# Row maxima by two heads at a time on half of the array, in a written-out cycle

## What is computed

```python
q = (x @ q_w + q_b).reshape(Bx, Tx, NH, HD).transpose(0, 2, 1, 3)
k, v = (kv[0], kv[1])
att = jnp.einsum('bhqd,bhkd->bhqk', q, k) * (1.0 / np.sqrt(HD))
att = att + build_alibi_bias(NH, Tx)[None]
att = jnp.where(causal[None, None], att, -jnp.inf)
att = jax.nn.softmax(att, axis=-1)
y = jnp.einsum('bhqk,bhkd->bhqd', att, v)
return y.transpose(0, 2, 1, 3).reshape(Bx, Tx, Cx) @ o_w + o_b
```

## Time and profile before

| | |
|---|---|
| median of 3 runs | 2727.81 us (2725.26 to 2729.4) |
| the profiled execution | 2729.97 us, span 2727.9 us |
| mean granted clock of TensorE | 0.978 |
| PE busy | 2598.3 us, 95% of the span |
| DVE busy | 2321.1 us, 85% |
| ACT busy | 2059.8 us, 76% |
| POOL busy | 1373.4 us, 50% |
| DMA | 299.58 MB moved, mean 110 GB/s |

### The profile page before, as it was taken

One profiled execution on the slowest core, in us unless ns is written; L12 is line 12 of the kernel. 1 busy time (PEld: TensorE's weight loads), 2 busy tenths in 40 slices (PEclk: granted clock), 3 DMA queues, 4 the chain that ended last, 5 costly groups with the idle time before them and its releaser, 6 DMA issues.

```text
span 2727.9 us, 57513 instructions
## 1 busy us (share of the span) xinstructions
PE 2598.3 (95%) x21670; PEld 1637.9 (60%) x21670; DVE 2321.1 (85%) x4175; ACT 2059.8 (76%) x3887; POOL 1373.4 (50%) x1768
## 2 busy tenths in 40 slices
PE   6779999999997999999999999999999999999998
PEld 4569989999996444545445454454544545455454
DVE  3468888888886998999989998899998999999993
ACT  2248878877884687888887887788887887887886
POOL 2235555555653365464654645546464464654644
PEclk9889999999998899999999999999999999999999
DMA  2015575545555646556474564655546556474540
GB/s 73 1 44 171 179 189 186 173 164 177 176 178 165 106 74 123 80 99 106 73 127 75 104 105 68 122 82 98 100 79 122 82 97 102 77 127 77 103 89 17
DMA packets 315172, 299.58 MB, mean 110 GB/s; under 512 B 97174, under 2 KB 265516, under 8 KB 314668
## 3 DMA queue, kind: packets, MB, share of 16 engines
q1 hardware_dynamic: 313344, 295.55, 50.9%
q10 hardware_dynamic: 1552, 0.36, 0.1%
HBM read 175.27 MB, written 120.06 MB: 108 GB/s over the span
## 4 chain that ended last, share of the span: by engine, by line
PE 54%; ACT 6%; DMA 5%; issue 1%; SPq 0%; DVE 0%; POOL 0%; POOLq 0%; ACTq 0%
PE t_y L1570 19%; PE t_r L1554 16%; PE t_a L1505 12%; ACT t_prob L1599 6%; DMA scr_m<-t_mrows 4%; PE t_a L1538 4%; PE t_r L1516 3%; DMA t_q<-scr_m 1%; DMA t_k<-t_blockb 0%; DVE t_mxc L1647 0%; ACT t_mrows L1616 0%; SPq L1411 0%; ACT t_near L1608 0%; SPq L1417 0%; POOL t_prob L1744 0%
## 5 line engine op out<-in xcount | busy, mean ns | idle before, releaser
L1599 ACT ACTIVATE t_prob<-t_r 128x512 f32<-128x512 f32 (+1 forms) x2432 | 1261.4, 599 | 289.5 <-PE t_r L1554 285.4
L1647 DVE TENSOR_REDUCE t_mxc<-t_a 128x1 f32<-128x512 f32 (+3 forms) x1920 | 1129.3, 643 | 105.4 <-PE t_a L1505 102.7
L1554 PE MATMUL t_r<-t_q,t_k 109*128 109x128 bf16 (+4 forms) x4608 | 831.7, 275 | 31.1 <-DMA t_q<-scr_m 20.9
L1505 PE MATMUL t_a<-t_k,t_q 99*128 99x512 bf16 (+3 forms) x2560 | 650.1, 320 | 1.5 <-DVE t_mxc L1647 1.0
L1750 POOL TENSOR_SCALAR_AFFINE_SELECT t_near<-t_near 128x512 f32<-128x512 f32 x512 | 332.7, 650 | 532.3 <-ACT t_near L1608 532.1
L1570 PE MATMUL t_y<-t_prob,t_v 128*32 128x512 f32 (+3 forms) x6144 | 588.0, 496 | 0.0
L1554 PEld LDWEIGHTS t_r<-t_q,t_k 102*128 102x128 bf16 (+1 forms) x4608 | 373.6, 98 | 342.9 <-ACT t_prob L1599 133.1
L1744 POOL TENSOR_SCALAR_AFFINE_SELECT t_prob<-t_prob 128x512 f32<-128x512 f32 x512 | 322.5, 637 | 276.9 <-ACT t_prob L1599 276.9
L1608 ACT COPY t_near<-t_r 128x512 f32<-128x512 f32 x512 | 307.5, 602 | 82.6 <-PE t_r L1516 65.6
L1505 PEld LDWEIGHTS t_a<-t_k,t_q 99*128 99x128 bf16 x2560 | 210.8, 98 | 228.5 <-DVE t_mxc L1647 155.0
L1570 PEld LDWEIGHTS t_y<-t_prob,t_v 128*32 128x32 f32 x6144 | 157.7, 109 | 257.3 <-issue 182.4
(11 more groups left out here) (199 smaller groups left out, 4129.2 us busy)
## 6 DMA issues: line engine op xcount, KB each, us to landing
t_q<-scr_q SPq DMA_DIRECT2D x384, 128.0 KB, 4.0
t_k<-scr_k SPq DMA_DIRECT2D x384, 128.0 KB, 6.6
scr_q<-j_part SPq DMA_DIRECT2D x96, 256.0 KB, 3.4
scr_k<-j_part SPq DMA_DIRECT2D x96, 256.0 KB, 2.5
scr_v<-j_v SPq DMA_DIRECT2D x32, 544.0 KB, 5.0
t_v<-scr_v SPq DMA_DIRECT2D x64, 272.0 KB, 8.1
p_x<-in_x SPq DMA_DIRECT2D x32, 512.0 KB, 4.3
scr_res<-j_x SPq DMA_DIRECT2D x32, 512.0 KB, 3.8
```

The lines of the kernel that those rows point to most:

```text
L1505: mm = pe.matmul(abank[n % A_BANKS][:, x * w:(x + 1) * w], q_op[t % NG][0:KA, h0 + x, i * P:(i + 1) * P], k_op[t % NG][0:KA, h0 + x, k0:k0 ...
L1554: mm = pe.matmul(ring[n % RING_BANKS][:, s * w + lo:s * w + hi], k_op[g][0:deep, h0 + s, j * P:(j + 1) * P], q_op[g][0:deep, h0 + s, q0 + ...
L1599: nc.scalar.activation(prob[:, q % SLOTS, h0:h0 + m, 0:w], ring[n % RING_BANKS][:, 0:m * w].rearrange("p (h n) -> p h n", h=m), ACT.Exp).t ...
L1647: V.tensor_reduce(mxc[:, t % 2, k0 // 512, h0:h0 + m, i], abank[n % A_BANKS][:, 0:m * w].rearrange("p (h n) -> p h n", h=m), AX.X, ALU.max ...
```

## The change

In `attend`, and in what the earlier stages lay ready for it:

- **Max and diag become one.** `q_max` and `k_max` are new operands: heads 0 and 1 of the group on partitions 0 to 62, heads 2 and 3 on 64 to 126. They hold three position rows, three of the six products of parts (48 rows, NMAIN = 51) and 12 rows of marks (NMAX = 63), whose product gives a large negative number where a key lies behind its query. A unit is a pair of matmuls, one for each half of the array's rows, into two banks of PSUM, and one reduction of up to 1024 elements. A group has 19 units: 15 of 1024 elements and 4 of 768. No copy by ACT, no select by POOL, no reduction from SBUF.
- **PSUM:** two slots of two banks for the maxima, in place of three of one; three banks in the ring, in place of four.
- **The maxima rows** go through ACT's own queue: `lift` issues the write, `spread`, some exponents later, waits for it to land and issues the read.
- **scale** goes from DVE to POOL; join is one operation, not two.
- **Order:** PE follows `CYCLE`, a table of 73 pieces that is run through once for each group (the four `out` once for each batch). `late` is how many periods a piece stands behind. The costs are used for the other engines' order only.
- **Loads:** three sets of operands, not four. q, k and v as before (12 transfers of 128 KB and one of 272 KB in a group), plus `q_pos` and, for the maxima, 12 transfers of 64 KB. The first group's are issued in `project`, 38 transfers in place of 18. `prepare` builds the marks on POOL.

```diff
-A_BANKS, RING_BANKS, SLOTS = 3, 4, 6
+A_SLOTS, RING_BANKS, SLOTS = 2, 3, 6
+BUFS = 3
+CYCLE = (
+    ("exp", 25, 9), ("exp", 26, 9), ("weigh", 2, 9), ("weigh", 3, 9), ("rows", 0, 8), ("exp", 27, 9),
...
             def largest(t, u, n):
-                i, k0, w, h0, m = MAX_UNITS[u]
-                if u == 0:
-                    operands_in(t)
+                pieces, pair = MAX_UNITS[u]
+                if first_max[t] == n:
+                    pe.wait_ge(s_qk[t % BUFS], 16 * (MARKS + MAX_LOADS * (t // BUFS + 1)))
                 free_slot(n)
...
+                        for depth, lo, hi in ((NMAIN, 0, far), (NMAX, far, w)):
+                            if lo < hi:
+                                for e in range(2):
+                                    mm = pe.matmul(abank[n % A_SLOTS][:, 512 * e + at + lo:512 * e + at + hi],
+                                                   q_max[t % BUFS][64 * e:64 * e + depth, h, i * P:(i + 1) * P],
+                                                   k_max[t % BUFS][64 * e:64 * e + depth, h, k0 + lo:k0 + hi],
+                                                   start=True, stop=True)
...
-                nc.scalar.copy(mrows[:, :], abank[n % A_BANKS][:, :].bitcast(BF16)[0:3 * GH * QT, 0:P]).then_inc(s_al, 1)
+                nc.scalar.copy(mrows[:, :], abank[n % A_SLOTS][:, 0:512].bitcast(BF16)[0:3 * GH * QT, 0:P]).then_inc(s_al, 1)
+                act.wait_ge(s_al, t + 1)
+                act.dma_start(scr["m"][t % NG], mrows[:, :]).then_inc(s_mw, 16)
+
+            def spread(t):
+                act.wait_ge(s_mw, 16 * (t + 1))
+                if t >= BUFS:
+                    act.wait_ge(s_pv, NQ * (t - BUFS + 1))
+                act.dma_start(q_op[t % BUFS][KA:KB, :, :].rearrange("p h t -> p (h t)"),
+                              scr["m"][t % NG].rearrange("(s n) q -> s (n q)", s=3)).then_inc(s_m[t % BUFS], 16)
```

More of the change, by code:

```diff
@@ L99, in prepare @@
         ones = sb("p_ones", [P, P])
+        marks = [sb(f"p_mark_{n}", [MSUB, P]) for n in "qk"]
         ldT = sb("p_ldT", [100, 4])
@@ L1174, in settle, with cyclic @@
                 e[4](end)
+def cyclic():
+    order = []
+    for period in range(min(e[2] for e in CYCLE), GROUPS + max(e[2] for e in CYCLE)):
+        for place, (kind, x, late) in enumerate(CYCLE):
+            t = period - late
+            if 0 <= t < GROUPS and (kind != "out" or t % NG == NG - 1):
+                order.append((period + place / len(CYCLE), kind, t // NG if kind == "out" else t, x))
+    return order
 def plan():
-    lead, lag = 1.5, 0.12
     pl = Planner()
-    width = [KEY_QUADS[r][3] * per_bank(KEY_QUADS[r][3]) for r, h0 in PIECES]
@@ L1196, in plan @@
-    streams = {n: list(reversed(s)) for n, s in streams.items()}
     slot_freed, ring_freed = [], []
     def maxima_in(t):
-        if all(("max", t, u) in pl.done for u in range(NU)) and all(("reduce", t, i) in pl.done for i in range(QT // 2)):
-            pl.give("DVE", max(pl.when("reduce", t, i) for i in range(QT // 2)), t - lead + 1, ("join", t, 0), 320,
-                    lambda end: pl.give("POOL", end, t - lead + 1, ("split", t, 0), 1250))
-    def selected(t, i, end):
-        if i % 2 == 1:
-            pl.give("DVE", end, t - lead + 0.5, ("reduce", t, i // 2), 1141, lambda end: maxima_in(t), "reduce")
+        if all(("max", t, u) in pl.done for u in range(NU)):
+            pl.give("DVE", max(pl.when("max", t, u) for u in range(NU)), t - 0.5, ("join", t, 0), 180,
+                    lambda end: pl.give("POOL", end, t - 0.5, ("split", t, 0), 1250))
@@ L1208, in weighted, with lifted @@
+    def lifted(t, end):
+        pl.issue.append((end, "lift", t, 0))
+        pl.give("ACT", end + 4000, t - 0.5, ("spread", t, 0), 330)
     def weighted(t, c, end):
@@ L1212, in inverted @@
         def inverted(end):
-            pl.give("DVE", end, t + 0.5, ("scale", t, c), 370, scaled)
+            pl.give("POOL", end, t + 0.5, ("scale", t, c), 720, scaled)
         def swapped(end):
-            pl.give("DVE", end, t + 0.5, ("invert", t, c), 290, inverted)
+            pl.give("DVE", end, t + 0.5, ("invert", t, c), 220, inverted)
         pl.give("DVE", end, t - 0.5, ("swap", t, c), 620, swapped)
@@ L1290, in plan @@
             slot_freed.append(("lift", t, 0))
-            pl.give("ACT", now + 165, rank, ("lift", t, 0), 200, lambda end, t=t: pl.order["SP"].append(("lift", t, 0)))
+            pl.give("ACT", now + 165, rank, ("lift", t, 0), 530, lambda end, t=t: lifted(t, end))
         elif kind == "exp":
@@ L1309, in plan @@
                 weighted(t, LAST_QUAD.index(x), now + 180)
-            if x == NQ - 1 and t + NG < GROUPS:
-                pl.order["SP"].append(("load", t, 0))
+            if x == NQ - 1 and t + BUFS < GROUPS:
+                pl.issue += [(now + 3000 * z, "load", t, z) for z in range(LOAD_PIECES)]
         elif kind == "out":
```

437 lines of the change are left out of this document (221 added, 216 removed).

## The result

The changed kernel takes 2766.09 us (median of 4, 2755.74 to 2772.86), the kernel before on the same chip 2728.61: 1.013 times as long, 95% interval 1.0089 to 1.0171. The forecast was 2654, 2.7% less, with a range of 2575 to 2745. It was wrong, and on the wrong side. The profiled execution took 2762.49 us with a span of 2760.0. Of all executions in this document one, of experiment e6 (2918.57 us), was in a slower state of the chip and is left out of its ratio.

A forecast was written before the change was run, and what follows sets the result against it. TensorE was taken as the bound, with VectorE close behind. First lift at 922 us, 62 groups of 26.9 (25.99 of TensorE work plus 0.9 of waits), then 17.7, 31 and 15.5 gave 2654 us; range 2575 to 2745.

The forecast's parts named there:

- the rows' part: Maxima rows' write and read on ScalarE's queue: median write landed before the wait, 3.4 us against 4.2 us of exponents.
- a DMA share of at most 0.77: Transfers of a group: 3.6 MB in 26.9 us, 134 GB/s, sets this upper limit on the DMA engines' share.
- Rival C: Wait for the maxima write holds ScalarE 1.8 us if landing grows to some 6 us; 28.2 a group, 2735 us, chance 0.08.
- the one for all waits: Waits in a group: about 0.5 us for the maxima rows and 0.4 for banks, 0.9 in all (0 to 1.8).
- TensorE's sum: TensorE's own work for one group of the changed kernel, matmuls and array changes: 25.99 us.
- the 0.5 for narrow pairs: Maxima on TensorE: 0.5 us a group, between nothing and 1.1, for the 20 pairs that are 128 wide.
- Rivals A and B: Maxima on TensorE: changes to halves cost 0.24 us, 2852, chance 0.14; or halves don't run at once, 2870, chance 0.05.
- Its terms gave 26.54: TensorE's own work for one group of the kernel before: 26.54 us of the 28.38 a group took.
- 1.08 a group: TensorE in the kernel before: waits for maxima rows not yet back, 22.8 us in 600; about 0.5 expected after.
- Half of the matmul time that the halves save is given back in changes: TensorE, one group: max and diag fall from 7.92 to 3.96 us, while changes rise from 1.57 to 4.48.
- VectorE, ScalarE, GpSimd, start and end: Per group 23.7, 20.1 and 11.1 us for the three engines; first lift near 922 us, 46.5 from last lift to end.
- Transfers: Loads run more than one group ahead and stay hidden, but lengthen the maxima rows' transfers; 3.6 MB a group.

The follow-up runs named there:

- e6: e2 with both matmuls of each maxima pair in the upper half of the array's rows; 2872.29 us, ratio 1.051 to the kernel before.
- e9: Changed kernel with v loaded for the first three groups only and reused for all others; 2651.08 us, ratio 0.9708 to the kernel before.
- e2: Changed kernel with q, k, v and maxima operand loads issued only once the maxima rows' write has landed; 2650.36 us, ratio 0.9685 to the kernel before.
- e7: Changed kernel with the maxima rows' write and read issued by SyncE, behind the loads in its queue; 2694.81 us, ratio 0.9884 to the kernel before.
- e8: e7 with each q, k and v load moved behind the next group's rows in SyncE's list; 2620.47 us, ratio 0.9607 to the kernel before.
- e13: e8 with the residual's additions 12 us later in the list that orders GpSimd; 2601.2 us, ratio 0.9503 to the kernel before.
- e11: Kernel before, with the residual issued behind the next maxima rows and its additions 26 us later; 2692.72 us, ratio 0.9863 to the kernel before.

## Why the prediction was wrong

- **The step that failed** is in the rows' part: "A queue without bulk in front can give the least landing, 1.4 us", and then "So the median write has landed when ACT comes to the wait." I took the landing from a median over groups with idle and with full engines, and thought of the queue as what makes a write wait. The row that I quoted beside it, 7.3 us, was from a group with 2 MB in flight. The runs show that what is in the engines counts: 6.4 us with the loads ahead (after), 5.2 without v (e9), 2.0 with the loads behind (e2), 7.2 in SyncE's queue behind them (e7), 2.8 in that queue ahead of them (e8). I had worked out a DMA share of at most 0.77, measured 0.71, and didn't carry it to the one transfer that is waited for.
- **Rival C** was this mechanism, with a hold of 1.8 us a group and 28.2 us for the group; measured are 1.8 and 28.5. It had a chance of 0.08. The term of the sum that was mis-sized is the one for all waits, 0.9 us. TensorE from 1100 to 2500 us (columns of the earlier trace rows) in the kernel before, the changed one, e2 and e13:

```profile
1100.00:2500.00 1400.00, 1372.44 (x12498) 705.19 (x12496) 1283.91 (x2172) 1136.38 (x2368) 725.80 (x1133) 1.00 0.56 95
1100.00:2500.00 1400.00, 1308.75 (x12399) 545.29 (x12392) 1185.81 (x1275) 966.45 (x1961) 532.79 (x837) 0.97 0.73 126
1100.00:2500.00 1400.00, 1356.20 (x13198) 575.88 (x13194) 1257.86 (x1358) 1025.98 (x2086) 559.97 (x886) 1.00 0.79 133
1100.00:2500.00 1400.00, 1398.05 (x13636) 593.00 (x13629) 1296.09 (x1402) 1061.53 (x2158) 587.80 (x921) 1.00 0.82 137
```

| us a group | before | changed | e2 | e13 |
|---|---|---|---|---|
| a group | 28.27 | 28.50 | 26.69 | 25.92 |
| TensorE idle (1400 less PE busy, over the groups in 1400 us) | 0.56 | 1.86 | 0.83 | 0.04 |
| lost to the lower clock | 0.10 | 0.73 | 0.07 | 0 |
| what is left | 27.6 | 25.9 | 25.8 | 25.9 |

The third row is half of the time that TensorE was busy at the lower level, by the trace's clock records. So the waits cost 1.86 us and the clock that they bring down 0.73, 2.6 us together where the sum had 0.9. For the clock it had no term at all.
- **TensorE's sum,** 25.99 us, held: 25.8 to 25.9 are left in all three kernels of the last row. Partly by luck: the halves are right (e6), but a change to or from them costs 0.10, not 0.12, and the 0.5 for narrow pairs was hardly needed, so the terms give about 25.99 - 27 x 0.02 - 0.46 = 25.0. The other 0.9 are missing from the method. Part of it is in the exponents' matmuls: those with another of their kind behind them take 0.476 ns a column over 56 groups of e13, not 0.43, which makes 0.6 us for their 12569 columns; why, I don't know. Rivals A and B fall.
- **The kernel before was short by the same.** Its terms gave 26.54, and 27.6 are left. I closed that gap with 22.8 us in 600 of waits for the rows, 1.08 a group. But the two rows that I added, 13.0 on the weight loads and 9.8 on the matmuls, are the same stands seen twice: TensorE idled some 10 us for them, 0.5 a group, which fits e11's gain. So the change saves TensorE 1.7 us of its own work in a group, and not the 0.55 of the two sums; the gain of e13 over the kernel before, 2.35 us, comes mostly from there.
- **"Half of the matmul time that the halves save is given back in changes"** doesn't follow from the prediction's own terms: 4.48 less 1.57 is 2.91 of 3.96, three quarters.
- **VectorE, ScalarE, GpSimd, start and end** held within 0.6 us a group and some 2 us. A reduction of 1024 from PSUM takes 1.12 us from start to start, taken as 1.13. VectorE after, in order of time (groups of alike instructions):

```profile
1499.03 10.16 DVE L1716 TENSOR_REDUCE t_mxc<-t_a 128x2 f32<-128x1024 f32 x9 [2.60 <-PE t_a L1570]
1509.11 0.71 DVE L1729 STREAM_TRANSPOSE t_ysw<-t_y 128x512 f32<-128x512 f32 x1
```

- **The forecast** had little room for this wait and came to 2654; e2, which takes it away and keeps all else, has 2650, with 0.83 us of waits where the sum had 0.9. The sum fits a kernel that the order of the transfers didn't let run.
- **Transfers:** "Loads are ahead by more than one group and stay hidden, but they lengthen the rows' transfers." Both halves are true; the second had no term in the sum.

## What to carry to other kernels

In these runs a small transfer that someone waits for is priced by what the DMA engines hold at that moment, not by its queue or its median: look for its time of issue in the pieces of the DMA share. Put bulk that has a period of slack behind such a transfer, which here was worth 4.4% (changed kernel to e2). Let the wait stand on an engine that has nothing else to do, and when one transfer is moved, look what is last in that queue and who adds it up. Idle time of the weight loads and of the matmuls at one moment is one wait: don't add the two rows. And check a sum of costs on the kernel before it is trusted for the kernel after: here it was 1.1 us short.

## What the runs showed that I had not expected

- With the DMA engines full, a write of 24 KB alone in its queue took 6.4 us in the median, against 1.4 at the least, and 2.0 in the median of e2, where the loads follow it.
- TensorE's own part of a group, idle and low clock taken off, is within 0.1 us the same in the changed kernel, e2 and e13, though their times lie 6% apart.
- Pairs of 128-column matmuls in the two halves of the array start 0.057 us apart; in one half (e6) it is (1.00 - 0.10) / 8 = 0.11.
- The hold cost more than the idle time behind it, since TensorE's clock then stood at its lower level (0.50) for some time (6.8 us in the rows above): that took 0.73 us a group in the changed kernel, 0.07 us in e2.
